# Routed block of a two-layer sequence kernel: a new order of the work, the turns written out, and the last step of two normalisations on ScalarE

## The reference

```
out   = attention with weights sigmoid(sum of 5 sines of q.k), normalised by their sum
out   = layernorm(out @ Wo.T + bo) * gamma + beta
x1    = layernorm(x + out)                       # first layer
w     = x1 @ router_w + router_b                 # one weight per token
sel   = the 127 tokens with the largest w        # top_k(w, 128) without the last
proc  = transformer block over the selected tokens (rope, masked softmax, gelu), times w
y     = layernorm(x1 + (x1, with the selected rows replaced by proc))
```

## Time and profile before

| | us |
|---|---|
| median of 3 runs | 6987.33 (6981.92 to 6988.23) |
| the profiled execution | 6984.06 |
| its span | 6982.3 |
| PE busy | 6082.9 (87%) |
| DVE busy | 5882.5 (84%) |
| ACT busy | 5852.8 (84%) |
| POOL busy | 144.3 (2%) |
| prologue, from the first x_in to the first turn | 6093 to 6173.5 |
| first turn | 100.35 |
| the other six turns | 634.51 |
| epilogue | 73.94 |

### The profile page before, as it was taken

How to read it: one execution, slowest core, us unless ns; L and a number is a source line. 1 busy time by engine, 2 the same in 40 slices (tenths; PEclk the granted TensorE clock), 3 DMA queues, 4 the chain that set the end, 5 groups by cost and what they waited for, 6 DMA issues and landing times. The chain is left out here.

```text
span 6982.3 us, 129315 instructions
## 1 busy us (share of the span) xinstructions
PE 6082.9 (87%) x48057; PEld 4363.4 (62%) x48057; DVE 5882.5 (84%) x4549; ACT 5852.8 (84%) x5874; POOL 144.3 (2%) x217
## 2 busy tenths in 40 slices
PE   7499999999999999999999999999999999645555
PEld 4366666666666666666666666666666666434444
DVE  5299889988999889889998899889988888677775
ACT  1199999999999999999999999999999999611111
POOL 0000000000000000000000000000000000000000
PEclk9799999999999999999999999999999999866766
DMA  7422112221222122212221122112211111212120
GB/s 264 160 71 79 55 46 71 76 60 48 67 77 63 46 63 80 62 46 61 79 68 47 55 80 70 47 55 78 71 47 47 47 47 47 58 51 54 39 51 18
DMA packets 469586, 463.03 MB, mean 66 GB/s; under 512 B 163637, under 2 KB 351957, under 8 KB 467865
## 3 DMA queue, kind: packets, MB, share of 16 engines
q1 hardware_dynamic: 463512, 448.56, 21.2%
q0 software_dynamic: 5376, 5.30, 0.3%
HBM read 291.45 MB, written 162.14 MB: 65 GB/s over the span
## 5 line engine op out<-in xcount | busy, mean ns | idle before, releaser
L659 ACT ACTIVATE a_wave<-a_ps_turn 128x1024 f32<-128x1024 f32 x5120 | 4903.7, 1357 | 67.2 <-PE a_ps_turn L593 66.9
L593 PE MATMUL a_ps_turn<-a_q_r,a_k_r 64*128 64x512 f32 x20480 | 3382.2, 397 | 361.9 <-ACT a_wave L659 281.6
L676 DVE SCALAR_TENSOR_TENSOR a_weight<-a_wave,a_head_c,a_weight 128x2048 f32<-128x2048 f32 x1536 | 3612.8, 2352 | 81.2 <-DVE a_weight L676 0.5
L593 PE MATMUL a_ps_turn<-a_q_r,a_rounder 64*128 64x512 f32 x20480 | 3235.7, 391 | 4.8 <-issue 4.8
L593 PEld LDWEIGHTS a_ps_turn<-a_q_r,a_k_r 64*128 64x128 f32 x20480 | 1949.5, 184 | 1512.8 <-ACT a_wave L659 826.8
L593 PEld LDWEIGHTS a_ps_turn<-a_q_r,a_rounder 64*128 64x128 f32 x20480 | 1975.6, 185 | 242.6 <-issue 8.7
L676 DVE SCALAR_TENSOR_TENSOR a_weight<-a_wave,a_head_c 128x2048 f32<-128x2048 f32 x512 | 1203.3, 2350 | 561.6 <-ACT a_wave L659 561.6
L653 ACT ACTIVATE a_weight<-a_weight,a_head_c 128x2048 f32<-128x2048 f32 x512 | 1178.6, 2302 | 37.6 <-issue 32.4
L613 PE MATMUL a_ps_out<-a_weight,a_v_r 128*32 128x512 f32 x4096 | 546.3, 605 | 8.4 <-ACT a_weight L653 6.8
L613 PEld LDWEIGHTS a_ps_out<-a_weight,a_v_r 128*32 128x32 f32 x4096 | 80.6, 108 | 194.9 <-issue 184.2
L572 POOL COPY a_head_c<-a_table 128x5 f32 (+1 forms) x128 | 52.6, 412 | 5624.8 <-ACT a_weight L653 5624.8
(11 more groups left out here) (234 smaller groups left out, 2055.9 us busy)
## 6 DMA issues: line engine op xcount, KB each, us to landing
a_q_r<-qs_d SPq DMA_DIRECT2D x256, 320.0 KB
qs_d<-a_q_hl SPq DMA_DIRECT2D x224, 320.0 KB, 5.1
a_k_r<-k_d SPq DMA_DIRECT2D x512, 128.0 KB
a_q_r<-qs_d SPq DMA_DIRECT2D x256, 160.0 KB
k_d<-p_k_hl SPq DMA_DIRECT2D x8, 4096.0 KB, 12.8
a_k_r<-k_d SPq DMA_DIRECT2D x512, 64.0 KB
o_d<-a_out SPq DMA_DIRECT2D x512, 34.0 KB
num<-o_d SPq DMA_DIRECT2D x32, 512.0 KB
```

What stands on the lines that cost most here:

```text
L593: last = nc.tensor.matmul(ps_turn[slot_of(r, s, f)][:, half, :], exact(w(rows[half])), exact(q_r[rows[half], k, f, :]), start=(i == 0), st ...
L659: nc.scalar.activation(wave[:, s // 2 % 2, f, s % 2, :], ps_turn[slot_of(r, s, f)][:].rearrange("p a b -> p (a b)"), ACT.Sin, scale=TURN_I ...
L676: return v.scalar_tensor_tensor(both(weight[:, i, :, :]), both(wave[:, i % 2, f, :, :]), head_c[:, k, f:f + 1], to, ALU.mult, ALU.add)
```

## The change

Four edits, all inside `routed_block`:

- The loop over the seven turns is written out (`for b in range(B - 1)`) for PE, ACT, DVE and POOL. SP's own loop stays.
- VectorE's order at the head of a turn becomes: denominators, `hn`, sum of numerators, `draw_o(0)`, angles, `draw_o(1)`, moments of x1, `add_bias(0)`, threshold, root's reciprocal, `add_bias(1)`. TensorE spreads the second half right after the first draw, projects the token's q, k, v, then both halves of o one after the other; the second half's projection goes to banks 0 and 1, and the wait for `mix_added` goes. `total` and its reciprocal move behind the copy of `p_lo`.
- The dense rows are made on ScalarE, eight Identity activations with a scale (reciprocal deviation) and a bias (`shift[:, 0]`, minus mean times it) per partition. VectorE makes `shift` in one small instruction.
- x1 is made in the same way from `mix` and `shift[:, 1]`. On ScalarE it stands ahead of the Exp; VectorE waits for it ahead of L1262.

```diff
+        shift = sb("shift", [P, 2, LT])
...
             body(None, 0)
-            with eng.Fori(0, B - 1, 1) as b:
+            for b in range(B - 1):
                 body(b, b + 1)
...
-                                ins = mm(A[:, 2 + t // 2, (t % 2) * D:(t % 2 + 1) * D],
+                                ins = mm(A[:, 2 - 2 * half + t // 2, (t % 2) * D:(t % 2 + 1) * D],
...
                         spread_den(0)
+                        pe.wait_ge(S["ot_drawn"], 2 * front + 1)
+                        spread_den(1)
...
-                        pe.wait_ge(S["ot_drawn"], 2 * front + 1)
 
                         wait_pos(pe, S["ms1"], front)
                         project(0)
-                        spread_den(1)
+                        pe.wait_ge(S["ot_drawn"], 2 * front + 2)
+                        project(1)
...
-                    if front is not None:
-                        pe.wait_ge(S["ot_drawn"], 2 * front + 2)
-                        pe.wait_ge(S["mix_added"], 2 * front + 1)
-                        project(1)
...
                         run(trig[:], ang_r[:], ACT.Sin, "trig_ready")
+                        ready("dense_shift")
+                        act.wait_ge(S["dense_stored"], 16 * back + 16)
+                        for t in range(LT):
+                            ins = nc.scalar.activation(dense[:, t, :], x1[:, t, :], ACT.Identity, bias=shift[:, 0, t:t + 1], scale=spread[:, 2, t:t + 1])
+                        ins.then_inc(S["dense_ready"], 1)
...
                         run(spread[:, 1, :], spread[:, 1, :], ACT.Sqrt, "dev2")
+                        ready_f("x1_shift")
+                        if back is not None:
+                            ready("dense_ready")
+                        for t in range(LT):
+                            ins = nc.scalar.activation(x1[:, t, :], mix[:, t, :], ACT.Identity, bias=shift[:, 1, t:t + 1], scale=spread[:, 1, t:t + 1])
+                        ins.then_inc(S["x1_ready"], 1)
...
-                        step_f(v.tensor_tensor(flat(num[:, 0, :, :]), flat(num[:, 0, :, :]), flat(num[:, 1, :, :]), ALU.add))
...
+                    if front is not None:
+                        step_f(v.tensor_tensor(flat(num[:, 0, :, :]), flat(num[:, 0, :, :]), flat(num[:, 1, :, :]), ALU.add))
+                        draw_o(0)
...
+                    if front is not None:
+                        draw_o(1)
+                    if back is not None:
+                        moments_of(step, x1, 2, "dense_var", EPS_LN / 4)
+                    if front is not None:
+                        add_bias(0)
...
-                        for t in range(LT):
-                            ins = v.tensor_scalar(dense[:, t, :], x1[:, t, :], moments[:, 2, t, 0:1], spread[:, 2, t:t + 1],
-                                                  ALU.subtract, ALU.mult)
-                        ins.then_inc(S["dense_ready"], 1)
+                        v.scalar_tensor_tensor(shift[:, 0, :], moments[:, 2, :, 0], -1.0, spread[:, 2, :], ALU.mult, ALU.mult).then_inc(S["dense_shift"], 1)
...
-                        for t in range(LT):
-                            ins = v.tensor_scalar(x1[:, t, :], mix[:, t, :], moments[:, 1, t, 0:1], spread[:, 1, t:t + 1],
-                                                  ALU.subtract, ALU.mult)
-                        step_f(ins)
-                    if back is not None:
-                        ready("exped")
-                        step(v.tensor_reduce(total[:], logits[:, :, 0:KSEL], AX.X, ALU.add))
-
-                        step(v.reciprocal(inv_total[:].rearrange("p (n r) -> p r n", r=QH), total[:].rearrange("p (r n) -> p r n", r=QH)))
-                    if front is not None:
-
+                        v.scalar_tensor_tensor(shift[:, 1, :], moments[:, 1, :, 0], -1.0, spread[:, 1, :], ALU.mult, ALU.mult).then_inc(S["x1_shift"], 1)
+                    if front is not None:
+
+                        ready_f("x1_ready")
...
                         v.tensor_copy(probs_t[0:KSEL, 0:8, :].rearrange("p a b -> p (a b)"), flat(Bk[0:KSEL, 0:2, :])).then_inc(S["p_lo"], 1)
+                        step(v.tensor_reduce(total[:], logits[:, :, 0:KSEL], AX.X, ALU.add))
+
+                        step(v.reciprocal(inv_total[:].rearrange("p (n r) -> p r n", r=QH), total[:].rearrange("p (r n) -> p r n", r=QH)))
```

More of the change, by code:

```diff
@@ L783, in routed_block @@
                  "att_drawn mixed ms2 dev4 normed2 h2_turned h2_drawn up gelu_ready down var5 dev5 "
-                 "res_ready dense_stored scattered thr_ready xb_ready out_row_ready").split()
+                 "res_ready dense_stored scattered thr_ready xb_ready dense_shift x1_shift x1_ready out_row_ready").split()
         S = {n: sem("r_" + n) for n in names}
@@ L1151, in add_bias @@
                             ins = v.tensor_tensor(mix[:, 4 * half + 2 * n:4 * half + 2 * n + 2, :],
-                                                  A[:, 2 + n, :].rearrange("p (a b) -> p a b", a=2),
+                                                  A[:, 2 - 2 * half + n, :].rearrange("p (a b) -> p a b", a=2),
                                                   rows[:, 0, :].unsqueeze(1).broadcast_to([P, 2, D]), ALU.add)
@@ L1192, in body @@
                         v.tensor_scalar(out_row[:], ext_s[:, 1:2], base[:, 0, bass.ds(back, 1)], None, ALU.add).then_inc(S["out_row_ready"], 1)
-                        moments_of(step, x1, 2, "dense_var", EPS_LN / 4)
-                    if front is not None:
-                        draw_o(0)
-                        add_bias(0)
-                        draw_o(1)
-                    if back is not None:
                         ready("dense_dev")
                         step(v.reciprocal(spread[:, 2, :], spread[:, 2, :]))
-                        dve.wait_ge(S["dense_stored"], 16 * back + 16)
-                        for t in range(LT):
-                            ins = v.tensor_scalar(dense[:, t, :], x1[:, t, :], moments[:, 2, t, 0:1], spread[:, 2, t:t + 1],
-                                                  ALU.subtract, ALU.mult)
-                        ins.then_inc(S["dense_ready"], 1)
+                        v.scalar_tensor_tensor(shift[:, 0, :], moments[:, 2, :, 0], -1.0, spread[:, 2, :], ALU.mult, ALU.mult).then_inc(S["dense_shift"], 1)
                     if front is not None:
@@ L1327, in _ @@
                 batches(dve, body)
-FRONT_STEPS, BACK_STEPS = 48, 27
+FRONT_STEPS, BACK_STEPS = 47, 27
 CONST_LOADS = 16
```

## The result

The changed kernel takes 6890.58 us (median of 4 runs, 6887.95 to 6891.25) against 6986.45 (6981.92 to 6988.23): the ratio is 0.9863, 95% interval 0.9846 to 0.9880, 95.9 us less. I had forecast 6909 and a range from 6891 to 6926.

What follows compares the result with a forecast made beforehand. No engine is full; VectorE's waits in a relay with TensorE and the loop's gaps bound the routed block. Savings of 70.2 + 2.1 + 3 + 1 = 76.3 from 6984.06 give 6907.8, adjusted to 6909; range 6891 to 6926.

Steps and rivals of the forecast that it cites:

- The gap: VectorE's 21.5 us idle on "issue", six times ahead of L1169; writing out the loop removes it, fresh code costing nothing.
- the gap stays: Rival, chance 0.08: the idle ahead of L1169 is code fetch, not the jump; 21.5 us come back, 6930.
- slower: Rival, chance 0.03: fresh code for four engines stalls on fetch, 3.6 us each, four stalls a turn: 7010.
- Head of the turn: New order up to L1128: `hn` ends at 2.3, projections run unbroken, L1128 starts at 22.6 against 34.61, 12.0 us saved.
- the sum: Gains added: six turns 70.2 us, longer gaps 2.1, first turn 3, prologue and epilogue 1; 76.3 in all.
- the 5.2 us: VectorE's old time from L1181's end to first draw: rest of angles, three threshold instructions, moments of x1; kept unchanged.
- the block: GpSimd's L882 addition holding a VectorE instruction, as L1181 for 4.37 us; forecast to remain, but now while TensorE works.
- VectorE meanwhile runs into L882 at 8.3 and stands until 12.84: Step in the turn's head: GpSimd's addition holds VectorE's angles as before, but now during TensorE's projections.
- Dense rows on ScalarE: Eight Identity activations ahead of the mask's copy take 4.0 us (3.0 to 5.0); the mask pick makes things 1.0 late.
- x1 on ScalarE: Late in the turn: x1 takes 4.0 us, then one 1.28 load and Exp; L1277 starts at 63.4 against 75.06.
- First turn 3, prologue and epilogue 1: Gains outside the six turns: first turn reaches L1128 at 26.4 against 29.4, 3 us; prologue and epilogue together 1, estimated.
- more is won: Rival, chance 0.15: ScalarE's eight take 3.0, mask not late, Exp's load falls elsewhere; 14 us a turn, 6891.

Runs made afterwards that it cites:

- the kernel of the old order without gap and block: Kernel before, order kept, with its seven turns written out and GpSimd's L882 started only after the first draw: 6917.69 us, ratio 0.9907.

## Why the prediction was right or wrong

- *The gap.* Right: no "issue" ahead of L1179 in any turn, and inside the turns only the one that is the wait for `spread_den`; fresh code cost nothing. On top of the new order it gave 23.8, priced at 21.5. Alone it gives 47. The rivals "the gap stays" and "slower" are out. The Trainium skill, "Runtime: NRT & Kernel Launch", section "Instruction fetch mechanics", says that a taken branch to code outside what has been fetched stalls until that code is there; the six gaps with the loop and none without it agree. That the gap is this fetch, and not other work of the jump, no run here shows.
- *Head of the turn.* Right in mechanism: `hn` at 2.0 (2.3), first draw 5.9 (6.4), the projections unbroken. L1138 was forecast at 22.6 and stands at 21.1 in the four held turns. The term of the sum that was mis-sized, and the largest part of the miss, is the 5.2 us that I carried over from L1181's end to the first draw. It held four angle instructions, but the block now falls later in the list and leaves none to three; and it held 0.24 of idle ahead of L1192 in the old turn that the new one doesn't have. It measures 4.4, reciprocal and shift 0.3 instead of 0.5, and the hold ends at 12.7 instead of 12.84. About 1.4 a turn, 8 in six turns.
- *The step that failed outright* is "VectorE meanwhile runs into L882 at 8.3 and stands until 12.84". I took it as certain in every turn. It holds in four of six. By my own walk the first draw ended at 7.9 and the eight angles, 0.2 each, would be over at 9.5, and L882 depends on the landing of the scatter; the turn of the old trace with the latest landing has it at 9.88 after zero, past the angles. A rival "L883 comes too late" was in the data and I didn't price it: 3.1 us for each free turn (92.0 against 88.9), 6 here. With the head's 8 and a tail shorter by 0.3 a turn, 2 in six, this makes up the 16 us by which the six turns beat the sum. How many turns come out free is luck of the landing: the traces with this placement have none, one or two.
- *Price of the block.* I let it stand "while TensorE works", as hidden behind the projections. TensorE was done at 18.9 and VectorE reached the second bias only at 19.9, and the delay ran on through ScalarE's dense rows and the mask's copy: a held turn is 3.1 longer. Held back, the addition gives 21 us (6869.4 against 6890.6), about half of it in those turns; the other half, in prologue and first turn, I had carried over from the old kernel as it was.
- *Dense rows on ScalarE.* Eight in 4.04, forecast 4.0. That it came out is in part luck: by the rows the step from 2048 columns to 256 leaves 0.44 and not 0.5, and no row had the second pointer or the overlap. Behind them the mask's copy, forecast late by 1.0: L1138 to L1255 takes 25.4 in held turns, forecast 25.4. In free turns it takes 23.6, less than the 24.4 of the old turn, so there nothing is late. Without the lateness (dense rows later on ScalarE) L1238 comes 0.5 earlier in held turns and 1.0 later in free ones, where TensorE turns q and k at the lower level.
- *x1 on ScalarE.* Right: 4.04, then one load of 1.28, then the Exp; L1255 to L1279 is 15.4, forecast 15.4. The drain of some 1.38 us that the Trainium skill ("ScalarE: Activation LUTs", section "What ACT_TABLE_LOAD costs") adds to a load isn't there: the load starts 0.01 after x1's last activation ends, and the Exp 1.30 after the load's start, 0.02 after its end. That x1 on ScalarE costs time stays likely and unproved, 5 to 9 us with overlapping runs.
- *First turn 3, prologue and epilogue 1.* Measured 4.6, 0.3 and 0.1. With the 3 us of the earlier start this is the rest of the miss: 96.5 of span against 76.3.
- *The range.* Its low end held the case "more is won" by other terms (a fast ScalarE) that did not occur; the case that did occur, a shorter head and two free turns, was not in it.

## What to carry to other kernels

When an instruction in a relay is held by a neighbour on a shared resource, price both the hold and what the next engine loses by the pause, and look in all turns of the trace how the two are placed: a start that hangs on a DMA's landing makes two kinds of turns, and a forecast should carry both. Before large reorderings, try the one wait that keeps the long GpSimd instruction out of a stretch where VectorE is late: here it was worth 45 us by itself. Gains of such edits don't add: here an edit that gave 45 to 69 us alone gave 10 to 45 as the second, and 21 to 48 as the third.

## What the runs showed of the hardware

- A GpSimd addition of 4.5 us with SBUF inputs holds a 128x8 VectorE instruction of 0.17 us until the addition ends, whether `tensor_scalar` (L1195, 4.40) or `scalar_tensor_tensor` with two SBUF inputs (L1181, 4.36); the eight statistics (one SBUF input) run beside it in the usual 2.71. The Trainium skill, "SBUF — State Buffer", section "Who interferes with whom", says that an instruction with at most one SBUF input outside the two-port modes doesn't contend; by that rule the statistics are the right neighbour for the addition, and the trace agrees. In the first turn L1180 is held for 5.23 although it starts 0.6 ahead of the addition's recorded start, beside the indirect DMA that GpSimd issues just before; with the addition held back the same instruction takes 0.23 beside the same DMA.
- The jump back of a loop costs 3.0 to 4.5 us on VectorE at its first instruction, six times of six in each of the four traces with the loop; written out, no turn shows it.
- The same sixteen passes of the projection take 3.72, 5.41 and 6.74 us after 0.70, 3.22 and 4.97 us of idle. The pause right ahead doesn't decide it alone: with the same 1.55 us of idle ahead `spread_den` took 2.05 or 3.78, and in the kernel of the old order without gap and block the projection took 5.41 in one turn (granted clock 0.66) and 3.72 in the next (1.00) after nearly equal pauses. What else does is left open.

```profile
6470.64 5.41 PE L941 MATMUL A<-woa_t,o_t 128*128 128x256 f32 x16 [2.75 <-DVE o_t L1164]
...
6569.27 3.72 PE L941 MATMUL A<-woa_t,o_t 128*128 128x256 f32 x16 [2.67 <-DVE o_t L1164]
```
